# Value products of a fused transformer layer: eight short visits per step turned into four joined ones

## The reference

```
h = concat(pos_table, nest_table[nesting], seg_table[segments]) @ W
h = h + attention(layernorm(h))
h = h + experts(layernorm(h))
```

## Time and profile before

| | |
|---|---|
| median of 3 runs | 1141.84 us (1139.55 to 1142.68) |
| the profiled execution | 1142.55 us |
| its span, first to last instruction | 1140.8 us |
| busy: PE / DVE / ACT / POOL | 91% / 84% / 71% / 60% |
| mean granted TensorE clock | 0.96 of full speed |
| maxima by DVE (L1023) | 1024 x 680 ns |
| exp by ACT (L591) | 1024 x 596 ns |
| value matmul instructions (L736) | 2048, in 256 calls |

### The profile page before, as it was taken

How to read it: one execution, slowest core, us unless ns; L and a number is a source line. 1 busy time by engine, 2 the same in 40 slices (tenths; PEclk the granted TensorE clock), 3 DMA queues, 4 the chain that set the end, 5 groups by cost and what they waited for, 6 DMA issues and landing times.

```text
span 1140.8 us, 20263 instructions
## 1 busy us (share of the span) xinstructions
PE 1041.5 (91%) x6158; PEld 403.4 (35%) x6158; DVE 962.6 (84%) x2442; ACT 805.1 (71%) x1578; POOL 682.6 (60%) x684
## 2 busy tenths in 40 slices
PE   5378999999999999999999999999999999999965
PEld 3112233333333333333334333333333333333323
DVE  7499889999899899899999999989999989788312
ACT  2217777777777777777777787777777777777841
POOL 1955677667666666676666676676666666632231
PEclk8559999999999999999999999999999999999997
DMA  2564645555555445655554455555554455541111
GB/s 70 150 141 100 139 102 125 131 133 128 121 135 122 116 118 124 142 124 131 126 128 118 120 122 130 134 127 120 136 120 120 115 127 137 119 103 46 49 60 35
DMA packets 93530, 132.43 MB, mean 116 GB/s; under 512 B 18205, under 2 KB 69918, under 8 KB 87398
## 3 DMA queue, kind: packets, MB, share of 16 engines
q1 hardware_dynamic: 91872, 129.54, 46.7%
q10 hardware_dynamic: 1550, 1.59, 0.5%
HBM read 89.20 MB, written 35.01 MB: 109 GB/s over the span
## 4 chain that ended last, share of the span: by engine, by line
PE 78%; DVE 8%; issue 4%; DMA 2%; ACT 1%; POOL 1%; SPq 0%; POOLq 0%; DVEq 0%; ACTq 0%
PE mix L749 20%; PE pv L736 20%; PE sc L723 16%; PE mix L803 9%; DVE negmax L1023 3%; PE mix L824 3%; PE mix L786 3%; PE mix L808 2%; DVE qk L1008 2%; DVE h_sb L1000 2%; PE mix L761 1%; PE mix L768 1%; PE mix L793 1%; DMA wrow<-w_dram 1%; ACT probs L591 1%
## 5 line engine op out<-in xcount | busy, mean ns | idle before, releaser
L1023 DVE TENSOR_REDUCE negmax<-mix 128x1 f32<-128x512 f32 x1024 | 667.0, 680 | 63.4 <-PE mix L749 57.8
L591 ACT ACTIVATE probs<-sc 128x512 f32<-128x512 f32 x1024 | 566.2, 596 | 181.2 <-PE sc L723 177.8
L749 PE MATMUL mix<-kstk,qstk 96*128 96x512 bf16 x1024 | 359.3, 394 | 50.7 <-DVE h_sb L1000 21.1
L723 PE MATMUL sc<-qstk,kstk 120*128 120x512 bf16 x1024 | 363.6, 382 | 1.2 <-ACT probs L591 0.8
L736 PE MATMUL pv<-probs,vals 128*32 128x512 f32 x2048 | 273.9, 601 | 0.2 <-ACT ctx_sb L615 0.2
L749 PEld LDWEIGHTS mix<-kstk,qstk 96*128 96x128 bf16 x1024 | 97.0, 98 | 388.4 <-DVE negmax L1023 173.2
L527 POOL TENSOR_TENSOR ctxh<-ctx_sb,rdenb 128x512 f32<-128x512 f32 x64 | 81.0, 1268 | 200.8 <-DMA rdenb<-rden_dram 200.5
L723 PEld LDWEIGHTS sc<-qstk,kstk 120*128 120x128 bf16 x1024 | 99.5, 98 | 110.6 <-ACT probs L591 42.8
L803 PE MATMUL mix<-xn2T,fc1T_sb 128*128 128x512 f32 x256 | 132.5, 600 | 0.7 <-ACT hid L645 0.7
L507 POOL TENSOR_TENSOR qk<-qk,rstdb 128x512 f32<-128x512 f32 x64 | 81.6, 1276 | 76.7 <-DMA rstdb<-rstd_dram 76.7
L645 ACT ACTIVATE hid<-mix 128x512 f32<-128x512 f32 x128 | 76.2, 595 | 35.8 <-PE mix L803 35.8
(11 more groups left out here) (141 smaller groups left out, 1089.4 us busy)
## 6 DMA issues: line engine op xcount, KB each, us to landing
stack_dram<-pieces SPq DMA_DIRECT2D x192, 128.0 KB
rdenb<-rden_dram SPq DMA_DIRECT2D x64, 256.0 KB
qstk<-stack_dram SPq DMA_DIRECT2D x31, 384.0 KB, 6.6
kstk<-stack_dram SPq DMA_DIRECT2D x31, 384.0 KB, 8.7
rstdb<-rstd_dram SPq DMA_DIRECT2D x32, 256.0 KB, 3.4
wrow<-w_dram SPq DMA_DIRECT2D x32, 256.0 KB
out<-out_sb SPq DMA_DIRECT2D x32, 256.0 KB, 2.5
qstk<-stack_dram SPq DMA_DIRECT2D x31, 256.0 KB, 6.9
```

Source lines behind the costliest of these rows:

```text
L591: act.activation(probs[:, c % 8, i % 2], sc[:, i % RING], ACT.Exp).then_inc(s_exp, 1)
L723: pe.matmul(sc[:, i % RING, :], kstk[0:KROWS, u, h, j * P:(j + 1) * P], qstk[0:KROWS, u, h, :], start=True, stop=True).then_inc(s_score, 1)
L749: pe.matmul(max_bank(m), qstk[0:STK, u, h, j * P:(j + 1) * P], kstk[0:STK, u, h, :], start=True, stop=True).then_inc(s_mxmm, 1)
L1023: dve.tensor_reduce(negmax[:, m // NT, m % NT:m % NT + 1], max_bank(m), AX.X, ALU.max, negate=True).then_inc(s_max, 1)
```

## The change

The eight calls of `values` per step, one in each odd slot, become four pairs: in slots 3, 7, 11 and 15 both values of `jj` are issued one behind the other. Within all slots the order is now M0, S0, product, S1, values, M1, so the visit lies ahead of the second max tile. The products `low` and `gates` (slots 3 and 7) are issued right before the visit, `mT` (slot 11) right behind it. In DVE's list `add_pos`, the first `stats1` and `weigh` all go to place 1 of slot 3, `finish` to place 1 of slot 7, the second `stats1` and `moments1` to slot 6, the first gate part to place 0 of slot 9 and the other three to place 1 of slot 10, and the second `add_qk` and `hot` to place 1 of slot 15. ACT makes both `qk` at the head of slot 4. In POOL's list one `second` goes ahead of `rstd1`. SP's list, the tiles, the number of instructions and the order in which banks rotate stay as they are.

```
-PE_ORDER = [("max", 0), ("scores", 0), ("product", 0), ("scores", 1), ("max", 1), ("values", 0)]
+PE_ORDER = [("max", 0), ("scores", 0), ("product", 0), ("scores", 1), ("before", 0), ("values", 0), ("behind", 0), ("max", 1)]
-BESIDE = (3, 7, 11)
+BEFORE, BEHIND = (3, 7), (11,)
 ACT_WORK = [
-    (1, 1, "relu", -3, 3), (1, 2, "qk", 3, 0), (3, 1, "qk", 3, 1), (4, 0, "ctx", -1, 1), (5, 2, "xn2T", -2, 0),
-    (8, 0, "gates", -2, 0), (9, 0, "gate_exp", -2, 0), (9, 1, "relu", -2, 0), (10, 1, "relu", -2, 1),
+    (1, 1, "relu", -3, 3), (4, 0, "qk", 3, 0), (4, 0, "qk", 3, 1), (4, 0, "ctx", -1, 1), (6, 0, "xn2T", -2, 0),
+    (8, 0, "gates", -2, 0), (9, 1, "gate_exp", -2, 0), (9, 1, "relu", -2, 0), (10, 1, "relu", -2, 1),
 DVE_WORK = [
-    (3, 0, "add_pos", 4, 0), (4, 0, "weigh", -3, 0), (4, 1, "stats1", 4, 0), (5, 0, "stats1", 4, 1),
-    (6, 0, "moments1", 4, 0), (6, 1, "finish", -3, 0), (7, 1, "invert_den", -1, 0),
-    (8, 1, "gate", -2, 0), (9, 1, "gate", -2, 1), (10, 0, "gate", -2, 2), (10, 0, "gate", -2, 3),
-    (13, 0, "add_qk", 4, 0), (15, 0, "add_qk", 4, 1), (15, 2, "hot", 5, 0),
+    (3, 1, "add_pos", 4, 0), (3, 1, "stats1", 4, 0), (3, 1, "weigh", -3, 0), (6, 0, "stats1", 4, 1),
+    (6, 1, "moments1", 4, 0), (7, 1, "finish", -3, 0), (7, 1, "invert_den", -1, 0),
+    (9, 0, "gate", -2, 0), (10, 1, "gate", -2, 1), (10, 1, "gate", -2, 2), (10, 1, "gate", -2, 3),
+    (13, 0, "add_qk", 4, 0), (15, 1, "add_qk", 4, 1), (15, 1, "hot", 5, 0),
 POOL_WORK = [
-    ("second", 3, 0), ("residual", 3, 0), ("third", 3, 0), ("rstd1", 4, 0),
-    ("second", 3, 1), ("residual", 3, 1), ("third", 3, 1), ("normalise", -1, 0), ("v", 3, 0),
+    ("second", 3, 0), ("residual", 3, 0), ("third", 3, 0), ("second", 3, 1), ("rstd1", 4, 0),
+    ("residual", 3, 1), ("third", 3, 1), ("normalise", -1, 0), ("v", 3, 0),
                     for what, i in PE_ORDER:
-                        if what == "values" and c in BESIDE and t > -4:
+                        if (what == "before" and c in BEFORE or what == "behind" and c in BEHIND) and t > -4:
                             product(t, c)
-                        if what == "product" and c not in BESIDE:
+                        if what == "product" and c not in BEFORE + BEHIND:
                             product(t, c)
-                        if what == "values" and c % 2 == 1:
-                            r, jj = c // 4 - 1, c // 2 % 2
-                            if r >= 0 and runs(t):
-                                values(t, r, jj, u)
-                            if r < 0 and runs(t - 1):
-                                values(t - 1, 3, jj, (u - 1) % U)
+                        if what == "values" and c % 4 == 3:
+                            r = c // 4 - 1
+                            for jj in range(2):
+                                if r >= 0 and runs(t):
+                                    values(t, r, jj, u)
+                                if r < 0 and runs(t - 1):
+                                    values(t - 1, 3, jj, (u - 1) % U)
```

## The result

The changed kernel takes 1128.95 us (median of 5, 1126.86 to 1132.64) against 1141.84 us (5 runs) before: ratio 0.9894, 95% interval 0.9876 to 0.9913. It is 1.1% faster, where 3.4% was forecast. The sign is right; the size is a third of the forecast, and the time lies 1 us above the stated range. The profiled execution takes 1126.86 us, 15.7 less than the one before.

The account below looks back on a forecast made before the run. PE plus two waits for DVE (`add_qk`, `add_pos`) was taken to set the step. 26 full steps at 1.3 us (33.8) and six lighter ones (5.4) off 1142.55 us gave 1103.4, so 1103; range 1084 to 1128, chance 0.8.

Parts of the forecast that it names:

- Six lighter steps: Steps 0 to 2 and 29 to 31: joined visits alone gain 0.9 us each, 5.4 us in all.
- The walk of a full step: PE and DVE carried through slots 0 to 15: 30.9 us, taken as 31.0 against 32.3; chance 0.45 (1095 to 1112).
- The short bank waits of slots 3 to 9: PE waits briefly for banks that DVE frees, among them 0.28, 0.16 and 0.12 us.
- `invert_den` "done by 15.5": Slots 4 to 7: DVE has `finish` and `invert_den` done by 15.5 us, then idles 0.8 us.
- the joint `qk` of ACT: Both `qk` at the head of slot 4, piece stores going out with them: costs nothing.
- The join: Paired value visits in slots 3, 7, 11, 15: each saves PE 0.235 us, 0.94 us a step.
- The rule on weight loads: The second group's loads would lie bare, 0.26 us a pair, so the join saves nothing; 0.235 was taken instead.
- The third, slower one: DVE idles behind each joined visit, lengthening the step: 1156 us at 0.8 us per visit, 1177 at 1.0; chance 0.10.
- 0.67 us of idle time per visit: DVE's 2.66 us of idle time per step, spread over four visits; idling beyond it lengthens the step.
- the second rival: Half the gain is lost to bare second-group weights or a late `load_max`: 1121 us; chance 0.26 (1112 to 1135).
- `load_max`: SP's load is issued up to 1.7 us later; slot 0's S0 might wait 0 to 0.7 us a step; nothing taken.

Follow-up runs that it names:

- third kernel: The changed kernel with the gate parts and `gate_exp` back at their old, earlier places (slots 8 to 10): 1120.47 us, ratio 0.9818.
- fourth: The changed kernel with `invert_den` one place later on DVE, ahead of M0 of slot 8: 1124.75 us, ratio 0.985.
- eighth: The changed kernel with gate parts 1 to 3 one slot later (slot 11, place 1): 1245.14 us, ratio 1.0933.
- seventh: The third kernel with PE's order, separate visits and DVE and ACT lists of before in all steps but 3 to 28: 1111.07 us, ratio 0.9744.
- tenth: The changed kernel in steps 3 to 28, with the old order, visits and lists in all lighter steps: 1118.41 us, ratio 0.9806.
- sixth: The third kernel with `den_out` ahead of the two piece stores in SP's list: 1118.15 us, ratio 0.9804.
- ninth kernel: The seventh kernel with `den_out` ahead of the piece stores in steps 3 to 28 alone: 1108.86 us, ratio 0.9722.
- first kernel: The kernel before the change, with `values` calls joined behind M1 and all lists as they were: 1192.51 us, ratio 1.0447.

## Why the prediction was wrong, and where it was right

The forecast gain was 39.2 us on the profiled execution, the measured one 15.7. The missing 23.5 us are 14.4 in the light steps and the fill and drain (11.2 in steps 29 to 31, 3.7 up to step 3, less 0.5 behind), and 9.1 in the full steps.

- **The step that failed: "Six lighter steps (0 to 2, 29 to 31), where DVE has room but the two adds are rarer, at 0.9 us each, the joins alone: 5.4."** I took the light steps for smaller full steps, and did not walk them. Steps 29 to 31 lost 8.5 us, and the start 1.0. The runs show two causes. The larger is the collision of `gsm`, `gad` and `wsafe` with POOL's `normalise` in step 29: 2.6 us of PE wait and 1.7 us of clock. It comes from the gate parts' later places on DVE: with the gate parts early it is gone from step 29, though `mT` is still behind the visit (third kernel); with POOL's `normalise` a little later it is gone too (fourth); and with the gate parts one slot later still it is in most steps (eighth). Step 30 has a smaller one (`gsel` 1.27 us, 0.85 us of PE wait). The prediction costed the move of the gate parts at DVE's time alone and named no other engine's instruction beside it. The smaller is ACT, which starves in a joined visit and then holds PE where few max tiles stand between the scores; with the old order and lists in the light steps alone the three steps have their old times (seventh). No run changes ACT's part by itself, so its share rests on the waits: 2.2 of the 3.5 us. Of the 3.7 us that are missing up to step 3, 2.6 are the new order and lists in the light steps (tenth against the changed kernel); the other 1.0 stays open.
- **The walk of a full step: nearly right.** It gave 30.9 and I took 31.0. The shortest steps of the changed kernel are 31.18, and 30.98 with the gate parts early. Stretch by stretch, from visit to visit, it had 8.67, 7.21, 7.51 and 7.52 us; the step of 580.30 to 611.50 shows 8.65, 7.28, 7.82 and 7.45. The one miss, 0.31 us, is in slots 8 to 11. The gate parts are a small part of it: with them early this stretch is still 7.73 at its shortest, and the next is 0.12 shorter. Half of it is `mT`, 0.42 us from its start to M1 where the walk has 0.27. The short bank waits of slots 3 to 9 came where the walk had them, by the starts on PE: 0.24 us at M0 of slot 3, 0.15 at `xn2T` and 0.15 at `fc1_0`, for 0.28, 0.16 and 0.12.
- **`invert_den` "done by 15.5": mis-sized.** The walk took its transfer as landed. In 25 of the 26 full steps DVE waits for it, 1.0 us on average and up to 1.6. Most of that is idle time under the visit of slot 7, as in the walk; the rest makes steps uneven, (31.35 − 31.18) × 26 = 4.4 us of the 9.1. The store leaves right behind the two piece stores that the joint `qk` of ACT had moved there, which I had costed at nothing: from its issue to that of the load it is 4.5 us at the median, 3.2 before and 3.4 with the store first. With it first, nearly all steps are 30.99 us (sixth and ninth kernel). The sixth kernel, with early gate parts as well, averages 31.02: these two account for 8.5 of the 9.1 us.
- **The join: right at PE, and it was not the term that I thought.** Before, a single visit took 0.10 us in and 0.99 to the next max tile; the joined one of slot 15 takes 0.09 and 1.86, which saves 0.23 us, where the prediction has 0.235. But alone it costs 1.6 us a step (first kernel), and on the new lists it is worth 1.4.
- **The rule on weight loads.** I had weighed the Trainium skill's page "TensorE: Matmul & The Clock Gate", section "Part 3: Packing small matmuls — row/col tiling", by which a load overlaps matmuls in flight only where its row group differs. Here both groups use all 128 rows. A joined visit of 1.84 us, less 0.11 to 0.14 for the way out, leaves 0.86 us for each group, and the second group's loads stand at 593.08, while the first computes. The measurement decides against the rule for this form. The same section also lets a load go ahead where it targets the background weight buffer; no run here shows whether that is what happens.
- **The rivals.** The third, slower one did not come for the change, but it is what the join alone does: 0.67 us of idle time per visit was the bound, and there it is 0.76 to 1.31. The measured time lies in the second rival's part of the range (1112 to 1135), but neither of its mechanisms occurred: the second group's weights are hidden, and no wait of PE in the full steps ends with a transfer, as one for `load_max` would. That rival came near by luck.

## What to carry to other kernels

Price a schedule in its light steps too: an order that fits a full step can lose where one engine's work is missing, and here 6 light steps took back 9.5 of the 24.7 us that the full steps gained. When an operation moves in time, look at which other engine's operations it will then run beside, above all VectorE's with two SBUF operands beside GpSimd's. A joined, denser visit pays only if the other engine's work is moved under it in the same edit, and neither half can be judged alone.

## What the runs showed of the hardware

- A VectorE operation of 16 columns on two SBUF operands, or `tensor_scalar` from and to SBUF, takes 0.17 us by itself and up to 1.27 us when a GpSimd `tensor_tensor` of 1.28 us is running: it ends when that one ends, and the next may be held by the next. A `tensor_reduce` (0.17 us) or a reciprocal (0.18 to 0.20) beside it is not held. The Trainium skill, page "SBUF — State Buffer", section "SBUF: two separate sides", says that the shared port pair is an exclusive lock, not a bandwidth split, taken by a VectorE operation in a two-port mode or, against a GpSimd operation that reads SBUF, by one with two SBUF inputs. With that rule the traces agree: beside `ctxh`, which reads SBUF, `gsm` takes 1.27 and `gad` 1.26 us, and `wsum`, with a single input, 0.17.
- The price of the lock is not the delay of the held operation but what is queued behind it elsewhere: 2.9 us on VectorE became 2.6 us of TensorE wait, and the granted clock of 0.68 over the 5.4 us behind it cost an estimated 1.7 us more.
- Two groups of four 128 x 32 f32 products, one behind the other, take 0.86 us each without a gap, the second group's weights being loaded while the first computes (loads at 593.08 us, matmuls from 592.64 and 593.50).
